# Between the scan and the expert tiles: where the weight remainders are formed, and in which steps the row addresses are

## The reference

```
x = x + tanh(g_xattn) * ssm(ctx_1024, z=layernorm(x))
def step(state, xs):                       # 256 steps, state [b, 256, 16]
    dA = exp(d_t[..., None] * A)
    state = state * dA + (d_t * u_t)[..., None] * B_t[:, None, :]
    y_t = einsum('ben,bn->be', state, C_t)
logits = einsum('td,de->te', xn, gate_w)   # xn = layernorm(x), 1024 rows, 8 experts
top_logits, top_idx = top_k(logits, 2); top_w = softmax(top_logits)
for e in range(8):
    h = silu(xn @ w0[e]) * (xn @ w1[e])    # 256 -> 512
    out = out + cw[:, e:e+1] * (h @ wo[e]) # 512 -> 256
x = x + tanh(g_ffn) * out
```

## Time and profile before

| | |
|---|---|
| median of 3 runs | 309.64 us (308.74 to 309.74) |
| the profiled execution, its own time | 307.61 us |
| its span in the profile | 305.8 us |
| TensorE busy | 265.8 us (87%) |
| VectorE busy | 229.0 us (75%) |
| ScalarE busy | 188.4 us (62%) |
| GpSimd busy | 183.2 us (60%) |
| HBM read and written | 22.5 MB, 74 GB/s over the span |

### The profile page before, as it was taken

The page is one execution under the profiler, slowest core; times in us unless marked ns, Lnnn a source line. Parts: engine busy times, 40 slices in busy tenths (PEclk is TensorE's granted clock), DMA queues, the critical chain, the costliest instruction groups (busy, mean ns, idle before and its releaser), DMA issues.

```text
span 305.8 us, 4685 instructions
## 1 busy us (share of the span) xinstructions
PE 265.8 (87%) x1166; PEld 178.1 (58%) x1167; DVE 229.0 (75%) x398; ACT 188.4 (62%) x349; POOL 183.2 (60%) x162
## 2 busy tenths in 40 slices
PE   8984698789788999897889489999999999999970
PEld 8432243234234345363565357988889898888960
DVE  2839999997889999999899664656565665656640
ACT  1894577865765685768484844565665657566540
POOL 5000449996999898998590442355547465565442
PEclk9996979999999999999999778999999999999996
DMA  7699200000000000001059611123242332423222
GB/s 233 225 395 387 94 2 0 0 1 0 0 0 3 1 0 0 0 2 69 1 184 331 242 49 39 29 41 57 48 69 40 63 51 52 68 35 69 28 26 34
DMA packets 16659, 22.70 MB, mean 74 GB/s; under 512 B 2554, under 2 KB 10274, under 8 KB 16642
## 3 DMA queue, kind: packets, MB, share of 16 engines
q1 hardware_dynamic: 11456, 16.41, 15.2%
q0 software_dynamic: 4416, 6.03, 11.9%
q10 hardware_dynamic: 770, 0.06, 0.2%
HBM read 17.38 MB, written 5.11 MB: 74 GB/s over the span
## 4 chain that ended last, share of the span: by engine, by line
PE 54%; DVE 23%; issue 11%; ACT 6%; POOL 3%; POOLq 1%; DVEq 0%; ACTq 0%
PE PD L1025 11%; PE PZ L1061 11%; PE PU L1025 10%; PE PY L844 7%; DVE states L1216 6%; DVE states L1222 5%; PE PY L1047 3%; DVE u L1142 2%; POOL hC L411 2%; PE PZ L1016 2%; PE PU L823 1%; PE PU L830 1%; PE PU L752 1%; ACT PD L612 1%; DVE WO L1240 1%
## 5 line engine op out<-in xcount | busy, mean ns | idle before, releaser
L411 POOL TENSOR_TENSOR hC<-states,WO 128x512 f32<-128x512 f32 x63 | 79.5, 1272 | 19.6 <-DVE states L1222 9.2
L1222 DVE TENSOR_TENSOR_SCAN states<-PD,states 128x512 f32<-128x512 f32 x64 | 77.3, 1209 | 1.3 <-ACT PD L612 1.0
L844 PE MATMUL PY<-hC,ident 128*128 128x512 f32 x128 | 68.9, 623 | 7.2 <-POOL hC L411 6.9
L446 POOL DMA_INDIRECT out<-lg,y_at x23 | 36.4, 1581 | 49.3 <-ACT lg L718 41.9
L612 ACT ACTIVATE PD<-WO,Aneg 128x510 f32<-128x510 f32 x64 | 43.9, 688 | 18.2 <-DVE states L1222 15.5
L1216 DVE TENSOR_TENSOR states<-PU,WO 128x512 f32<-128x512 f32 x64 | 42.7, 668 | 2.7 <-POOL hC L411 1.6
L402 POOL TENSOR_TENSOR W_lo<-W,W_hi 128x512 fp32r<-128x512 f32 x25 | 32.5, 1308 | 11.5 <-ACT W_hi L523 11.5
L1459 DVE TENSOR_TENSOR dA<-PU,dA 128x512 f32<-128x512 f32 x23 | 15.9, 691 | 28.5 <-PE PU L1025 28.5
L702 ACT ACTIVATE hidT_hi<-PY 128x512 fp32r<-128x512 f32 x23 | 13.8, 598 | 38.0 <-PE PY L1047 38.0
L1471 DVE TENSOR_TENSOR WO_lo<-WO,WO_hi 128x512 fp32r<-128x512 f32 x46 | 29.7, 688 | 9.4 <-issue 9.3
L844 PEld LDWEIGHTS PY<-hC,ident 128*128 128x128 f32 x128 | 21.9, 191 | 23.4 <-POOL hC L411 17.3
(11 more groups left out here) (245 smaller groups left out, 507.2 us busy)
## 6 DMA issues: line engine op xcount, KB each, us to landing
W<-in_L_ffn_w SPq DMA_DIRECT2D x16, 512.0 KB, 10.9
WO<-in_L_ffn_wo SPq DMA_DIRECT2D x8, 512.0 KB, 8.4
xs<-in_x SPq DMA_DIRECT2D x2, 512.0 KB, 5.5
out<-xs SPq DMA_DIRECT2D x2, 512.0 KB, 3.2
x_rows<-u SPq DMA_DIRECT2D x2, 512.0 KB, 5.9
early<-in_ctx SPq DMA_DIRECT2D x1, 512.0 KB, 4.2
hC<-x_rows,x_at POOLq DMA_INDIRECT x23
out<-lg,y_at POOLq DMA_INDIRECT x23, 3.8
```

The costliest lines, as they stand in the source:

```text
L411: pool.tensor_tensor(hC[:, n % 2, :], states[:, n % RING, :], C_rep[:, pair % C_RING, :], ALU.mult).then_inc(hc_done, 1)
L446: pool.indirect_dma_start(out=out, out_offset=bass.IndirectOffsetOnAxis(ap=y_at[:, s:s + 1], axis=0), in_=y_tile[s % 2], in_offset=None, c ...
L844: pe.matmul(PY[:, h, :], ident[:, :], hC[:, n % 2, :], start=False, stop=(m == DS - 1)).then_inc(y_done, 1)
L1222: dve.tensor_tensor_scan(states[:, n % RING, :], DEC[n % 2], states[:, n % RING, :], 0.0, ALU.mult, ALU.add).then_inc(scan_done, 1)
```

## The change

The last 14 remainders are shared out anew: GpSimd forms four (right after the scan, as before) and then none; VectorE forms six, all after the slot table; TensorE four, without the wait for ScalarE's copy. Of the high parts, seven are made inside the scan, two before `x2_out(2)` and five after `x2_out(3)`. The places and slot numbers are compared as unsigned integers, without conversion to float32. `normed(1)` and the gap stand behind the first one-hot tile of slots, `normed(0)` before the last scan step. x_at is made in one instruction from TABLE (minus 1, at least 0) ahead of the splitting of the routing weights; for a place without a row that is row 0. y_at comes after two of the remainders. The expert counts have a bank and a semaphore of their own, `add_x(1, 1)` comes after the logits, and the first `x_turn` before the wait for the slot table. The first `gate` waits for two of VectorE's remainders, the first `up` for all six.

```diff
-UPPER_AT = (56, 57, 59, 60, 62)
-POOL_SPLITS = tuple(range(EARLY, EARLY + 4)) + tuple(range(EARLY + 9, EARLY + 12))
-PE_SPLITS = tuple(range(EARLY + 5, EARLY + 9))
-DVE_SPLITS = (EARLY + 4,) + tuple(range(EARLY + 12, len(SPLITS)))
+UPPER_AT = (50, 53, 56, 57, 59, 60, 62)
+POOL_SPLITS = tuple(range(EARLY, EARLY + 4))
+PE_SPLITS = tuple(range(EARLY + 6, EARLY + 10))
+DVE_SPLITS = tuple(range(EARLY + 4, EARLY + 6)) + tuple(range(EARLY + 10, len(SPLITS)))
...
-        rank_i = sb("rank_i", [P, NQ, TOPK, QBLK], I32)
-        row_i = sb("row_i", [P, NQ, TOPK, QBLK], I32)
-        row_f = sb("row_f", [P, NQ, TOPK, QBLK])
-        tile_i = sb("tile_i", [P, NQ, TOPK, QBLK], I32)
-        slot_of = sb("slot_of", [P, NQ * TOPK * QBLK])
+        rank_i = sb("rank_i", [P, NQ, TOPK, QBLK], U32)
+        row_i = sb("row_i", [P, NQ, TOPK, QBLK], U32)
+        tile_i = sb("tile_i", [P, NQ, TOPK, QBLK], U32)
...
+        COUNT = bank[5]
         TABLE = bank[3]
-        SPLIT = [bank[i] for i in (4, 0, 1, 4)]
+        SPLIT = [bank[i] for i in (4, 0, 1, 7)]
...
 @block.gpsimd
-            for i in POOL_SPLITS[:4]:
-                lower(i)
-            pool.wait_ge(row_f_ok, 1)
-            for i in POOL_SPLITS[4:]:
+            for i in POOL_SPLITS:
                 lower(i)
...
             pool.wait_ge(stored, 16 * NQ)
+            pool.wait_ge(y_at_ok, 1)
...
 @block.scalar
             normed(range(QBLK))
+            for i in range(EARLY + len(UPPER_AT), EARLY + 9):
+                upper(i)
             x2_out(2)
             x2_out(3)
-            for i in range(EARLY + len(UPPER_AT), EARLY + 9):
+            for i in range(EARLY + 9, len(SPLITS)):
                 upper(i)
             root(1)
             normed(range(QBLK, NBLK))
             act.wait_ge(gap_ok, 1)
             act.activation(egap[:, :], gap[:, :], ACT.Exp).then_inc(egap_ok, 1)
-            for i in range(EARLY + 9, len(SPLITS)):
-                upper(i)
...
 @block.tensor
                 pe.wait_ge(mask_sum, 1)
-                pe.matmul(RANKS[:, 0:E * NBLK], ones[:, :], upto[:, :, :].rearrange("p e t -> p (e t)"), start=False, stop=False)
-                pe.matmul(RANKS[:, E * NBLK:E * NBLK + E], ones[:, :], upto[:, :, NBLK - 1], start=False, stop=True).then_inc(rank_ps, 1)
+                pe.matmul(COUNT[:, 0:E], ones[:, :], upto[:, :, NBLK - 1], start=True, stop=True).then_inc(count_ps, 1)
+                pe.matmul(RANKS[:, 0:E * NBLK], ones[:, :], upto[:, :, :].rearrange("p e t -> p (e t)"), start=False, stop=True).then_inc(rank_ps, 1)
...
             through(ADD_NEXT_AT + 1, NT)
-            add_x(1, 1)
...
-                if j >= 3:
-                    pe.wait_ge(W_lo_act, j - 2)
...
             router(1)
+            add_x(1, 1)
             for r in range(QB):
                 add_gz(1, r)
...
-                pe.matmul(bank[5], ident[:, :], W1_hi[:, 0, 0, :].bitcast(F32), start=True, stop=True)
+                pe.matmul(TABLE, ident[:, :], W1_hi[:, 0, 0, :].bitcast(F32), start=True, stop=True)
...
-            pe.wait_ge(slots_ok, 1)
...
+            x_turn(0, 0, 16)
+            pe.wait_ge(slots_ok, 1)
             first = expert_of(0)
-            x_turn(0, 0, 16)
             pe.wait_ge(W_lo_pool, EARLY + len(POOL_SPLITS))
-            pe.wait_ge(W_lo_dve, len(DVE_SPLITS))
             pe.wait_ge(W_lo_act, len(PE_SPLITS))
+            pe.wait_ge(W_lo_dve, 2)
             gate(0, 0, first)
             x_turn(1, 1, 16)
+            pe.wait_ge(W_lo_dve, len(DVE_SPLITS))
             up(0, 0, first)
...
 @block.vector
             def rows_hot(j):
-                rf = row_f[:, :, :, :].rearrange("p q k t -> p (q k t)")[:, 4 * j:4 * j + 4].rearrange("p (n o) -> p n o", o=1).to_broadcast((P, 4, P))
+                rf = row_i[:, :, :, :].rearrange("p q k t -> p (q k t)")[:, 4 * j:4 * j + 4].rearrange("p (n o) -> p n o", o=1).to_broadcast((P, 4, P))
...
-                dve.wait_ge(rank_ps, 1)
+                dve.wait_ge(count_ps, 1)
...
                 need(starts)
+                dve.wait_ge(rank_ps, 1)
...
-                in_tile = mark(dve.tensor_scalar(row_i[:, :, :, :], rank_i[:, :, :, :], P - 1, None, ALU.bitwise_and))
+                dve.tensor_scalar(row_i[:, :, :, :], rank_i[:, :, :, :], P - 1, None, ALU.bitwise_and).then_inc(row_i_ok, 1)
                 slots = mark(dve.tensor_scalar(tile_i[:, :, :, :], rank_i[:, :, :, :], P.bit_length() - 1, None, ALU.logical_shift_right))
-                need(in_tile)
-                dve.tensor_copy(row_f[:, :, :, :], row_i[:, :, :, :]).then_inc(row_f_ok, 1)
                 need(slots)
-                link(dve.tensor_copy(slot_of[:, :], tile_i[:, :, :, :].rearrange("p q k t -> p (q k t)")))
...
-                dve.tensor_tensor(slot_w[:, 0, :, :], iota_c[:, :, :].to_broadcast((P, n, COLS)), wide(slot_of[:, :]), ALU.is_equal).then_inc(slot_hot_ok, 1)
+                dve.tensor_tensor(slot_w[:, 0, :, :], iota_c[:, :, :].to_broadcast((P, n, COLS)), wide(tile_i[:, :, :, :].rearrange("p q k t -> p (q k t)")), ALU.is_equal).then_inc(slot_hot_ok, 1)
...
+                normed(1)
+                dve.wait_ge(rstd2_ok, NQ)
+                dve.tensor_tensor(gap[:, :], gap[:, :], rstd[:, 1, :], ALU.mult).then_inc(gap_ok, 1)
                 rows_hot(0)
...
                 for j in range(1, 4):
                     rows_hot(j)
-                normed(1)
-                dve.wait_ge(rstd2_ok, NQ)
-                dve.tensor_tensor(gap[:, :], gap[:, :], rstd[:, 1, :], ALU.mult).then_inc(gap_ok, 1)
...
-            through(LOGITS_AT, NT)
+            through(LOGITS_AT, NT - 1)
+            normed(0)
+            through(NT - 1, NT)
...
             gated(1, 0)
             gated(1, 1)
-            normed(0)
-            lower(DVE_SPLITS[:1])
             logits_of(1)
...
             link(dve.tensor_tensor(wts[:, :, 1, :], wts[:, :, 0, :], by_q(egap), ALU.mult))
+            dve.wait_ge(table_ps, 1)
+            dve.tensor_scalar(x_at[:, :], TABLE[:, 0:COLS], -1.0, 0.0, ALU.add, ALU.max).then_inc(x_at_ok, 1)
...
-            dve.wait_ge(table_ps, 1)
-            link(dve.tensor_scalar(spare[:, :], TABLE[:, 0:COLS], 0.0, spare_id[:, 0:1], ALU.is_equal, ALU.mult))
-            dve.scalar_tensor_tensor(out=y_at[:, :], in0=TABLE[:, 0:COLS], scalar=-1.0, in1=spare[:, :],
-                                     op0=ALU.add, op1=ALU.add).then_inc(y_at_ok, 1)
-            dve.wait_ge(y_at_ok, 1)
-            dve.tensor_scalar(x_at[:, :], y_at[:, :], TOK - 1, None, ALU.bitwise_and).then_inc(x_at_ok, 1)
...
-            link(dve.tensor_reduce(slot_f[:, :], ended[:, :, :], AX_X, ALU.add))
-            link(dve.tensor_scalar(slot_f[:, :], slot_f[:, :], float(E - 1), None, ALU.min))
+            expert = mark(dve.tensor_reduce(slot_f[:, :], ended[:, :, :], AX_X, ALU.add))
+            empty = mark(dve.tensor_scalar(spare[:, :], TABLE[:, 0:COLS], 0.0, spare_id[:, 0:1], ALU.is_equal, ALU.mult))
+            need(expert)
+            expert = mark(dve.tensor_scalar(slot_f[:, :], slot_f[:, :], float(E - 1), None, ALU.min))
+            need(expert)
             dve.tensor_copy(slot_tab[:, :], slot_f[:, :]).then_inc(slots_ok, 1)
-
-            lower(DVE_SPLITS[1:])
+            lower(DVE_SPLITS[:2])
+            dve.scalar_tensor_tensor(out=y_at[:, :], in0=TABLE[:, 0:COLS], scalar=-1.0, in1=spare[:, :],
+                                     op0=ALU.add, op1=ALU.add).then_inc(y_at_ok, 1)
+            lower(DVE_SPLITS[2:])
```

More of the change, by code:

```diff
@@ L258, in build @@
         exp_done, dbu_done, scan_done, hc_done, y_done = map(sem, ("exp_done", "dbu_done", "scan_done", "hc_done", "y_done"))
-        row_f_ok = sem("row_f_ok")
+        row_i_ok = sem("row_i_ok")
         x_stored, row_hot_ok, slot_id_ok, table_ps, y_at_ok, x_at_ok = map(
@@ L268, in build @@
         W_hi_ok, W_lo_pool, W_lo_dve, xT_split = map(sem, ("W_hi_ok", "W_lo_pool", "W_lo_dve", "xT_split"))
-        W_lo_ps, W_lo_act, last_hc, mask_sum = map(sem, ("W_lo_ps", "W_lo_act", "last_hc", "mask_sum"))
+        W_lo_ps, W_lo_act, last_hc, mask_sum, count_ps = map(sem, ("W_lo_ps", "W_lo_act", "last_hc", "mask_sum", "count_ps"))
         w_hi_ok, w_lo_ok = sem("w_hi_ok"), sem("w_lo_ok")
@@ L1321, in rows_hot @@
             def rows_hot(j):
-                rf = row_f[:, :, :, :].rearrange("p q k t -> p (q k t)")[:, 4 * j:4 * j + 4].rearrange("p (n o) -> p n o", o=1).to_broadcast((P, 4, P))
+                rf = row_i[:, :, :, :].rearrange("p q k t -> p (q k t)")[:, 4 * j:4 * j + 4].rearrange("p (n o) -> p n o", o=1).to_broadcast((P, 4, P))
                 ri = iota_row[:, :].rearrange("p (o r) -> p o r", o=1).to_broadcast((P, 4, P))
-                dve.wait_ge(row_f_ok, 1)
+                dve.wait_ge(row_i_ok, 1)
                 dve.tensor_tensor(row_hot[:, 4 * j:4 * j + 4, :], ri, rf, ALU.is_equal).then_inc(row_hot_ok, 1)
@@ L1330, in places @@
                 n = NQ * TOPK * QBLK
-                dve.wait_ge(rank_ps, 1)
+                dve.wait_ge(count_ps, 1)
```

(2 more changed lines are left out.)

## The result

The changed kernel takes 304.85 us (median of 4 runs, 304.53 to 305.61), the kernel before 309.19 us in the same comparison; the ratio is 0.987, 95% interval 0.9837 to 0.9902. That is 3.0 to 5.0 us less, where 5.5 was forecast (304.1 us). The profiled execution took 304.53 us, its span is 302.7 us.

A forecast was written before the change was run, and what follows sets the result against it. The stage between scan and first expert tile, ahead of tiles that fill TensorE, was taken to decide the end: first `up` ends at 181.3 instead of 186.78 us, so 309.64 - 5.5 = 304.1 us; range 302.4 to 306.2.

The forecast's parts named there:

- Logits and counts: Router after the scan: logits end some 0.6 us earlier, but delayed ranks leave the counts at about the old time.
- Integer comparisons: VectorE's slot_w and four row_hot: comparing integers costs nothing extra; bounds 0 and 3.0 us.
- Five high parts before the root: ScalarE before root(1): 0.54 us each, from about 162.65 to 165.35, reciprocal roots at 165.75, before slot_w ends.
- The routing chain and x_at: Behind the one-hots: four small operations of 0.2 us; x_at at 171.1 instead of 176.61, a gain of 5.5 us.
- the second store of rows: SyncE's store ahead of the gather: issued at 168.3, landed at 172.2, so it comes last, not x_at.
- the two bounds of the text: Landing of SyncE's second store of rows: 171.1 us at the earliest, 177.2 at the latest.
- rival A: The store of rows lands later, each 1 us costing 1 us: 306.1 us with 2 more; chance 0.17.
- The clock: TensorE at the first `gate`: half clock again, six matmuls in 2.92 us, `gate` to end of `up` 4.65 us.
- rival B: Clock stays full at the first `gate`, VectorE then bounds: `up` ends at 180.3, time 303.1 us; chance 0.15.
- VectorE's remainders: Six remainders and y_at last until 177.75, `split_x` until 178.15, covered before `gate`'s fifth matmul at 178.6.
- Rival C: VectorE's slot_w products hold up GpSimd's gather by 0.6 us: 304.7, or 305.3 if two gathers count; chance 0.10.
- Rival D: Places without a row all read row 0, slowing gathers in the tiles: 8 us lost, 312.1 us; chance 0.04.

The follow-up runs named there:

- noisy: Changed kernel with three remainders back on GpSimd beside the one-hots, VectorE forming three instead of six: 308.14 us, ratio 0.997 to the kernel before.
- quiet_only: Kernel before with only GpSimd's last three remainders moved to VectorE, behind the slot table: 308.57 us, ratio 0.999 to the kernel before.
- late_norm: Changed kernel with `normed(1)` and the gap put back behind all one-hots: 306.23 us, ratio 0.9904 to the kernel before.
- act_store: Changed kernel with the second store of rows issued by ScalarE on its own queue, behind `egap`: 306.45 us, ratio 0.991 to the kernel before.
- early_wo_warm: The last experiment: changed kernel with three WO loads inside the scan and one extra matmul on either side of `x_turn`: 301.77 us, ratio 0.9776.
- norm0_back: Changed kernel with `normed(0)` back behind `gated(1,1)`: 306.13 us, ratio 0.9879 to the kernel before.
- rows_first: Changed kernel with the second store of rows ahead of the last two WO loads, ScalarE's wait for `stored` moved before its second tile: 305.85 us, ratio 0.9889.
- early_wo: Changed kernel with three of the eight WO loads moved into the scan: 302.56 us, ratio 0.9778 to the kernel before.

## Why the prediction was right, and where its sum was off

The direction, the place and most steps hold, and the time lies in the range.

- *Logits and counts.* Expected: logits 0.6 us earlier, counts at about the old time, as `add_x` now delays the ranks. The last logits came at 159.20 instead of 159.82, and from the end of the last scan the counts came after 8.15 us (162.47 - 154.32), before after 8.23. Right.
- *Integer comparisons*: free, as taken. *Five high parts before the root*: they ended at 165.2 (expected 165.35), the root was ready for `normed(1)`. The store was issued at 168.15 (168.3).
- *The routing chain and x_at*: 0.17 us each; x_at at 170.66 (171.1). Right, and noisy and quiet_only show the cause from both sides. But I priced x_at as if it were the only lock. TensorE's stream (low part 3 at half clock, weights' matmuls to 180.2) ended only 0.4 us ahead of `x_turn` in the kernel before, and ScalarE's copy of the turned rows (181.52) came 0.5 us behind it, held by that same low part. I had TensorE free at 175.2 after the change (it was 174.2), without saying that this was needed for the gain.
- *The step that failed: the second store of rows.* "I take 170.3 + 1.35 + 0.6 for completion = 172.2" was mis-sized. It landed at 173.8, and at 174.9 in the second profile: 5.67 and 6.69 us instead of 3.9. The 0.6 comes from no row. The 1.35 is one store's share of the stretch in which the earlier trace rows shows two, but here too the store of x is issued 0.4 us behind it (168.56) and moves with it: from 170.0 to 172.5 the DMA carried 383 GB/s, or 0.96 MB, about what both stores hold. And there is a tail, in the loads (0.31 of share was left at 170.5 before) and in the stores (0.36 at 172.5, 0.07 still at 174.0). No run leaves the store of x out, so how the 1.6 us divide between these stays open. The truth lay between the two bounds of the text, near their middle. late_norm and act_store show that neither issue time nor queue set the landing, early_wo_warm that the data ahead did. This is what rival A described, 1.6 to 2.7 us late. Issued 3.4 us earlier than before, the store landed 0.5 us earlier in one profile and 0.6 later in the other.
- *A slip in the sum.* 175.5 and its three terms (0.44, 0.36, 0.25) give 176.55, not 176.65.
- *A term left out: `normed(0)`.* The text gave its move no price. It took 1.01 us beside GpSimd's product in the first profile and 0.13 in the second, and norm0_back shows no loss; but the text had not asked.
- *The clock* fell before the first `gate`, as forecast (2.92 us), and rival B's price of it, 1.0 us, was 1.3 to 1.6 by the medians of the run that kept it up, and 1.7 from `x_turn` on in its profile.
- *VectorE's remainders* were expected to end just in time (178.15 with split_x). They ended at 176.91 and never bound, as the rows came later. With the store mended they do bind (177.05 to 177.46).
- *Rival C*, VectorE holding up the gather: the first gather took 1.38 us and the second, started at 175.79, took 1.95, but this was on no path; in the second profile they took 1.67 and 0.95, and in early_wo_warm one beside two remainders (173.22) took 0.96. No wait of 0.6 us that `x_turn` felt is shown. The Trainium skill (SBUF — State Buffer, "Who interferes with whom") says that a VectorE instruction with two SBUF inputs contends with a GpSimd instruction that reads SBUF, and not with one that only writes it. The trace agrees for GpSimd's remainders, which read SBUF (slot_w 1.65 us beside them against 0.56); for the gathers the durations above settle nothing.
- *Rival D*, the hot row: no wait for gathered rows within the tiles (TensorE waits for them once, at the first `x_turn`), and the spread addresses changed no time.

So the term of the sum that was mis-sized is the landing of the store. In the profile the first `up` ended at 183.67 against 181.3 in the sum, 2.4 us late: 1.7 at the start of the gather (174.11 against 172.4), 0.15 until its rows were there, 0.3 between `x_turn` and `gate`, mostly `x_turn` at half clock (0.70 against 0.44), and 0.2 in the beginning of `up`, still at half clock. The time came nearer, 304.85 us against 304.1, and that is partly luck: the two medians differ by 4.3 us where the two profiles differ by 3.1 (a second profile of the changed kernel: 0.7).

## What to carry to other kernels

When an engine works its stream in order, ask of the late step what stands ahead of it there, not only what it waits for: a wait three microseconds shorter is worth nothing if the stream comes free no earlier. A transfer that comes last is priced by all the data ahead of it and beside it, tail included, not by the moment at which the mean share falls; here issuing it sooner moved only its start, and moving other loads into an idle stretch moved its end. Before comparing one stage between two profiles, check that both had the same clock on the way to it. Three remainders on GpSimd cost VectorE about 1 us, nearly one of them (1.24), at each operation that met them, small or large.

## What the runs showed of the hardware that was not expected

- The clock fell to half while TensorE was working. In three of fourteen profiles (rows_first, early_wo, norm0_back) it was at 0.50 from about 160 to 163 us, right behind the router's matmuls of 8 columns; the stage then ran some 2 us late. In the other profiles, the changed kernel's two among them, it stayed at 1.00 there. What sets it off was not found; all three have `add_x(1, 1)` behind the router, but so have eight that did not fall.
- A like fall stands earlier in nine of the fourteen: about 3.5 us at 0.50, beginning between 147.5 and 150, behind the router's matmuls for the first half of the rows. In the first profile of the changed kernel it lasted from about 148 to 151.5. These nine are the ones whose first scan starts at 29.6 to 30.2 us; the five in which it starts at 30.6 or 30.7, those of before and of the changed kernel's second among them, have none. In the nine the product behind the last scan comes 124.7 to 124.9 us after the first scan, in the five 124.2 or 124.3, whatever the kernel.
- In the last experiment four runs with a mean granted clock of 0.974 to 0.976 took 301.4 to 301.8 us, and two with 0.964 took 303.3 and 303.4. At which place their clock fell is in no trace.
- A store of 512 KB took from 2.8 to 6.7 us to land (up to 10.7 for the first one, behind six loads), by what else was under way, and a gather of 128 rows from its start to `x_turn` 2.9 to 3.5 us where `x_turn` waited for it, and 5.5 beside two loads and a store.
